# A second cross-attention layer with stacked f16 score operands and f32 value products

## The chip, the cores and the metric

The kernel runs on one core of one Trainium2 chip, in one launch. The metric is the device time of that launch in microseconds (us). The kernel before takes 1686.76 us, the median of three runs from 1685.93 to 1686.81.

## The reference

Four layers, each with a cross-attention and a feed-forward part, act on x of 8 batch items by 256 tokens by 128 numbers. Each part adds its result to x, behind a layer norm. The context has 256 tokens of 96 numbers per batch item. The second layer's attention, which the change rewrites, has 16 heads of 8 numbers each:

```python
q = (q_tokens @ Wq.T).reshape(B, T_q, 16, 8).transpose(0, 2, 1, 3)
k, v = ...                       # the same from kv_tokens, 96 columns wide
attn = softmax(einsum('bhqd,bhkd->bhqk', q, k) / sqrt(8), axis=-1)
out = einsum('bhqk,bhkd->bhqd', attn, v).transpose(0, 2, 1, 3).reshape(B, T_q, 128)
return out @ Wo.T
x = x + _L1_xattn_ref(_layernorm(x), ctx_768, Wq, Wk, Wv, Wo)      # second layer
x = x + _L1_ffn_ref(_layernorm(x), ...)                            # 8 experts, one per token
```

All of it is in f32, and the kernel's f16 operands are pairs of a high and a low part.

## The kernel before, in words

The kernel is one program for each engine: TensorE (PE), VectorE (DVE), ScalarE (ACT), GpSimd (POOL) and SyncE (SP, which issues DMAs). All five walk the same lists of steps, written out by hand, and meet at semaphores (`need`). Layers are numbered from 0, so the second is `ATT[1]` and `FFN[1]`.

**The layer's passes.** `ATT[1]` works through the 8 batch items one after the other. Its kinds of pass are "early" (keys and values of all items, 512 columns at a time, put between the products of the first feed-forward's first chunk by `ffn_schedule`), "prologue" (the first three quarters of the queries), "first" (item 0), "mid" (items 1 to 6, a loop on every engine), "last" (item 7) and "epilogue". The fourth quarter of the queries is filled at head 4 of "first", behind "lastrows", the norm of the last 512 tokens. The first feed-forward has four chunks of 512 tokens and eight experts, and ends just before.

**One head.** `head_steps` gives every engine its order. In step i come the scores of head i, its softmax, the turn of head i-2, the low part of head i-3, the value products of head i-4, and in odd steps the norm of a pair:

```python
st = [("scores", i), ("softmax", i)] if i < 16 else []
st += [("turn", i - 2)] if i < 18 else []
st += [("low", i - 3)] if i < 19 else []
st.append(("av", i - 4))
if i % 2:
    st.append(("norm", (i - 4) // 2))
```

For the scores, PE multiplies the query, masked to the head's 8 rows of 128 (`Qz`, written by POOL in four masks per item, line 1147), with the whole key tile `kT`: two f32 products of 128 rows and 256 columns. DVE takes the negative maximum of each row (`negm`, line 2445), ACT the exponential (`Pm`, line 1491, in two halves). PE turns the four 128x128 blocks (line 1671). ACT copies the turned tile to f16 (`PTh`, line 1445), DVE subtracts that from the tile to get the low part (`PTl`, line 2456), and PE forms the value products in f16 from three pairings, (high, high), (high, low), (low, high): twelve of 9 columns, the ninth column being a one for the sum of the row. DVE divides by that sum (lines 2514 and 2516).

**Between the heads.** `NARROW` puts the previous item's output projection, residual (lines 2535 to 2539), layer norm and the choice and rank of its experts (lines 2594 to 2635) at fixed steps of the item. In "first" eight heads also carry a block maximum over the next feed-forward's weights (line 2336); their maximum (`uprow`, line 2421) goes to POOL, which reduces it over all partitions (line 1110), and DVE picks the result up at head 15 (line 2425). In "last" the weights are split in f16 parts (lines 1445 and 2463). SP loads the biases and weights of the next feed-forwards once the first feed-forward is done (line 917).

Of the kernel before, what the change touches and what calls it, by code (L numbers as in the profile page):

```python
# [9 lines left out]
F16 = mybir.dt.float16  # L10
# [8 lines left out]
P = 128  # L19
B, S, D = 8, 256, 128  # L20
T = B * S
# [39 lines left out]
class AttentionSems:  # L61
    def __init__(self, c):
# [7 lines left out]
        self.ctxb, self.qm, self.ostats, self.onorm = c["ctxb"], c["qm"], c["ostats"], c["onorm"]  # L70
# [156 lines left out]
def att_early(A):  # L227


    if A.dh != 64:  # L230
        return [(kind, j) for kind in "kv" for j in range(4)]
    return [("k", 0), ("k", 1)] + ([] if A.null else [("k", 2)]) + [("v", 0), ("vlow", 0), ("v", 2), ("vlow", 2)]


def att_prologue(A):

    return ([("sums", 0), ("srows", 0), ("tokens", 0)] if A.null else []) + [("q", 0), ("q", 1), ("q", 2)] + (
        [("sn", 0)] if A.null else [])
# [54 lines left out]
def on_act(A, kind, k, m):  # L293

    if A.dh != 64:
# [10 lines left out]
                (5, 1): ("v", 0), (6, 1): ("v", 1), (7, 1): ("v", 2), (8, 1): ("v", 3)}  # L306


def ffn_schedule(F, first):
# [3 lines left out]
    for e in range(F.E):  # L313
        if e * F.FT < F.U:
            for ft in range(F.FT):
                st.append(("up", (e, ft)))
                if F.n == 0 and first and (e, ft) in NEXT_CONTEXT:
                    st.append(("context", NEXT_CONTEXT[e, ft]))
                if F.k and e == 0 and ft == 1:
                    st.append(("gate", 1))  # L320
# [14 lines left out]
def build(nc, a, out):  # L335
    ctx = ExitStack()
    with ctx:
# [21 lines left out]
        headmask = sb("headmask", [P, 16])  # L359
# [43 lines left out]
        vmax = sb("vmax", [P, 4])  # L403
        vmaxall = sb("vmaxall", [P, 4])
# [28 lines left out]
        G = Qz[:, :, :].rearrange("p h s -> p (h s)").rearrange("p (g s) -> p g s", s=CH)  # L433
# [169 lines left out]
        out_written = sem("out_written")  # L603

# [40 lines left out]
        def att_counts(A):  # L645
# [3 lines left out]
            vfills = [m % 2 or A.dh == 64 for k in kinds if A.n != 2 for kind, j, m, _ in steps(A, 0, k) if kind == "v"]  # L649
            return dict(vhigh=sum(vfills), vlow=len(vfills) - sum(vfills), filled=fills, act=(fills + 1) // 2, dve=fills // 2, scores=nh, negmax=nh, exp=nh, dn=8 * B if A.null else 0, onull=8 * B if A.null else 0, xnb=B if A.null else 0,  # L650
                        turn=nh, pt0=nh // 2 if A.n == 2 else nh, pt1=nh // 2 if A.n == 2 else nh, av=nh, norm=nh if A.n == 2 else nh // 2, stats=B,
                        yn=B, numbers=B if A.n == 2 else 0, ctxb=B if A.dh == 64 else 0, qm=4 * B if A.n == 1 else 0,
# [99 lines left out]
        def batches(eng, A, body):  # L752
# [6 lines left out]
            with eng.Fori(1, B - 1) as b:  # L759
                body(b, "mid")  # L760
# [3 lines left out]
        def chunks(eng, F, body, behind_first=None, last=NCH):  # L764
# [3 lines left out]
            with eng.Fori(1, last) as c:  # L768
                body(c, False)

# [44 lines left out]

        def v_low(A, dve, k, src, b):
# [13 lines left out]

        kTall = kT[:, :, :].rearrange("p h s -> p (h s)")

        def keys_of(A, b, h):
            return kTall[:, bass.ts(b, S)] if A.n == 1 else kT[:, h, :]
# [80 lines left out]
        def _(sp):  # L915
# [56 lines left out]
            for n in ROUTED:  # L972
# [4 lines left out]
                for i in range(5):  # L977
                    sp.dma_start(xs[n][27 * P * i:27 * P * (i + 1), D:D + 1].bitcast(U32).rearrange("(t p) o -> p (t o)", p=P),
                                 unused[:, 27 * i:27 * i + 27], allow_slow_non_contiguous=True).then_inc(rows_set[n], 16)
            need(sp, ffn_s[0].y, NCH * FFN[0].E)  # L980
            load("b2", b2all, a["L1_ffn_b2"].rearrange("(o e) d -> o (e d)", o=1).to_broadcast([P, 8 * D]))
# [4 lines left out]
            load("l2f", n2, a["L2_ffn_w2"].rearrange("e d f -> d e f"))  # L986

# [50 lines left out]
        def _(pool):  # L1038
# [21 lines left out]
            for e in range(8):  # L1060
# [12 lines left out]
            link(pool.memset(headmask[:, :], 1.0))  # L1073
            link(pool.affine_select(out=headmask[:, :], in_=headmask[:, :], compare_op=ALU.is_ge, fill=0.0,
                                    base=0, pattern=[[-8, 16]], channel_multiplier=1))
            link(pool.affine_select(out=headmask[:, :], in_=headmask[:, :], compare_op=ALU.is_ge, fill=0.0,
                                    base=7, pattern=[[8, 16]], channel_multiplier=-1))
# [19 lines left out]
            pool.partition_all_reduce(vmaxall[:, 0:3], vmax[:, 0:3], P, RMAX).then_inc(setup_vmaxall, 1)  # L1097
# [36 lines left out]
            def attention(A, last_rows=None):  # L1134
# [6 lines left out]
                def masks(b, bw, heads=range(0, 16, 4)):  # L1141

                    for h in heads:
                        if b is not None:
                            need(pool, s.scores, b * 16 + (h + 4))
                        plain(pool)
                        pool.tensor_tensor(  # L1147
                            Qz[:, h:h + 4, :], xnT[:, bass.ts(bw, S)].unsqueeze(1).to_broadcast([P, 4, S]),
                            headmask[:, h:h + 4].unsqueeze(2).to_broadcast([P, 4, S]), ALU.mult).then_inc(s.qm.sem, 1)

                def body(b, kinds):
                    if A.n == 2:
# [13 lines left out]
                        pool.memset(R1[:, 5632:5648], 0.0)  # L1166
                        for c in range(3):
# [38 lines left out]
                    if A.n == 1 and kinds == "prologue":  # L1206

                        need(pool, s.ring.act, 5)
                        need(pool, ffn_s[0].y, NCH * FFN[0].E)
                        masks(None, 0, (0, 4))  # L1210
                        last_rows()
                        masks(None, 0, (8, 12))
# [11 lines left out]
                    if A.n == 1 and kinds == "first":  # L1224

                        need(pool, s.ring.act, 6)
                        need(pool, s.ring.dve, 6)
                        masks(0, 1)
# [1686 lines left out]
```

## Time and profile before

| | |
|---|---|
| runs | 1686.76 us median, 1685.93 to 1686.81 |
| the profiled execution | 1684.98 us, its span 1683.2 us |
| PE, its weight loads, DVE, ACT, POOL busy | 1401.7, 1083.9, 1133.7, 833.0, 396.2 us |
| granted clock, mean | 0.929 of full speed |
| the second layer's attention | about 578 to 890 us |
| one middle item of it | 33.7 us |

The span is the time from the first to the last instruction on the chip; the execution has 1.8 us around it. PE's clock has two levels, 1.2 and 2.4 GHz, and the profile gives the granted clock of a stretch as a share of the higher, so 0.50 is the lower level throughout. Busy shares of the whole span mix stages with different limits. The stage that counts here is the second layer's attention, and the rows below are mostly from it.

### The profile page before, as it was taken

The page shows a single profiled execution, that of the slowest core. Times are in us where ns is not written, and L with a number is a line of the kernel's source. Part 1 is how long each engine was busy: PE and PEld are TensorE (multiplying, and loading weights), DVE is VectorE, ACT ScalarE, POOL GpSimd, SP SyncE. Part 2 cuts the span into 40 slices and gives each one's busy share as a digit, 9 for nine tenths or more (in the row PEclk, how much of TensorE's full clock was granted, in tenths as well). Part 3 has the DMA queues.
Part 4 walks back from the last instruction along what each step waited for, and adds up shares of the span by engine and source line. Part 5 has one row for each costly group of instructions (what it writes and reads, how often), then busy time and mean ns, then how long its engine had stood idle before and what let it go on. Part 6 is the DMA issues. An engine that isn't in the chain of part 4 may idle for free. (4 is left out here: it accounts for less than half of the span.)

```text
span 1683.2 us, 38856 instructions
## 1 busy us (share of the span) xinstructions
PE 1401.7 (83%) x12529; PEld 1083.9 (64%) x12529; DVE 1133.7 (67%) x3284; ACT 833.0 (49%) x1838; POOL 396.2 (24%) x738
## 2 busy tenths in 40 slices
PE   3899999978999979998966864488868899898977
PEld 2677777765666658777754644366646677677665
DVE  4788888876766668888865454443357877788851
ACT  1666666654333346666642242322246665656633
POOL 2000000011111223433322324643311222222221
PEclk9999999988999989999978877699988999999989
DMA  8999100000000210000001100131110000000000
GB/s 228 279 98 132 0 0 0 0 1 1 1 1 0 68 49 5 3 3 6 4 4 43 35 27 17 41 102 43 35 52 1 2 0 0 0 0 0 1 1 25
DMA packets 109759, 55.06 MB, mean 33 GB/s; under 512 B 44593, under 2 KB 102578, under 8 KB 109474
## 3 DMA queue, kind: packets, MB, share of 16 engines
q1 hardware_dynamic: 106146, 46.53, 15.0%
q0 software_dynamic: 3520, 7.31, 1.3%
q8 instruction: 55, 0.90, 0.2%
q14 instruction: 38, 0.31, 0.1%
HBM read 27.09 MB, written 26.74 MB: 32 GB/s over the span
## 5 line engine op out<-in xcount | busy, mean ns | idle before, releaser
L1491 ACT ACTIVATE Pm<-bank,negm 128x256 f32<-128x256 f32 x528 | 220.8, 470 | 220.3 <-DVE negm L2445 122.6
L1667 PE MATMUL bank<-kT,Qz 64*128 64x256 f32 (+2 forms) x1568 | 309.6, 414 | 16.5 <-DVE negm L2436 4.7
L1671 PE MATMUL bank<-ident,Pm 128*128 128x128 f32 x1568 | 238.0, 288 | 63.6 <-DVE PTs L2456 58.3
L2456 DVE TENSOR_TENSOR PTs<-bank,PTs 128x512 f16<-128x512 f32 x384 | 251.4, 682 | 39.7 <-ACT PTs L1445 38.9
L1671 PEld LDWEIGHTS bank<-ident,Pm 128*128 128x128 f32 x1568 | 181.1, 146 | 140.9 <-issue 95.3
L1667 PEld LDWEIGHTS bank<-kT,Qz 64*128 64x128 f32 (+1 forms) x1568 | 189.7, 194 | 99.2 <-issue 57.4
L1445 ACT ACTIVATE PTs<-bank 128x512 f16<-128x512 f32 (+1 forms) x388 | 215.5, 590 | 3.8 <-PE bank L1671 3.7
L1667 PEld LDWEIGHTS bank<-VxF,PTs 128*128 128x128 f16 (+1 forms) x4672 | 183.3, 100 | 11.6 <-DVE PTs L2456 3.2
L1667 PE MATMUL bank<-VxF,PTs 128*128 128x65 f16 (+3 forms) x4672 | 187.4, 189 | 2.1 <-DVE PTs L2456 1.9
L1491 ACT ACTIVATE Pm<-Pm,negm 128x256 f32<-128x256 f32 x256 | 109.7, 497 | 117.2 <-DVE negm L2436 90.0
L2445 DVE TENSOR_REDUCE negm<-bank 128x2 f32<-128x512 f32 x136 | 93.5, 688 | 47.5 <-PE bank L1667 44.2
L1667 PE MATMUL bank<-Qz,R 128*128 128x128 f16 x978 | 93.1, 235 | 22.3 <-ACT Qz L1445 13.7
L2436 DVE CUSTOM_DVE_ANT_0 Pm<-bank,mb 128x256 f32<-128x256 f32 x256 | 93.5, 420 | 18.7 <-PE bank L1667 17.9
L1667 PEld LDWEIGHTS bank<-Qz,R 128*128 x978 | 71.7, 102 | 48.9 <-issue 37.0
L2442 DVE TENSOR_REDUCE negm<-bank 128x2 f32<-128x512 f32 x128 | 88.1, 689 | 19.9 <-PE bank L1667 18.9
L1667 PE MATMUL bank<-xHL,R 128*128 (+1 forms) x432 | 99.5, 379 | 1.4 <-DVE Qz L2850 1.2
L1147 POOL TENSOR_TENSOR Qz<-xnT,headmask 128x1024 f32<-128x1024 f32 x32 | 60.7, 1899 | 161.9 <-PE bank L1667 123.2
L1667 PE MATMUL bank<-xnT,R 128*128 (+2 forms) x288 | 87.3, 433 | 8.1 <-DVE VxF L820 6.1
L1667 PEld LDWEIGHTS bank<-R,Qz 128*128 128x128 f32 x704 | 83.8, 192 | 11.1 <-ACT Qz L1643 6.4
L1636 ACT ACTIVATE Pm<-bank,upback 128x512 f32<-128x512 f32 x72 | 49.4, 687 | 82.3 <-PE bank L1667 77.1
L1667 PE MATMUL bank<-R,Qz 128*128 128x128 f32 x704 | 85.0, 276 | 3.1 <-ACT Qz L1643 3.1
L1378 POOL DMA_INDIRECT expert_rows_by_token<-PTs,Qz x62 | 60.6, 977 | 110.3 <-DVE PTs L2764 66.6
(331 smaller groups left out, 2160.5 us busy)
## 6 DMA issues: line engine op xcount, KB each, us to landing
token_rows_by_expert<-trash SPq DMA_DIRECT2D x10, 1782.0 KB, 18.6
Qz<-token_rows_by_expert SPq DMA_DIRECT2D x62, 66.0 KB, 1.8
R<-expert_rows_by_token SPq DMA_DIRECT2D x12, 256.0 KB, 4.6
R<-in_L_ffn_ew SPq DMA_DIRECT2D x2, 1024.0 KB, 7.3
R<-in_L_ffn_w SPq DMA_DIRECT2D x1, 2048.0 KB, 9.5
R<-in_L_xattn_Wkv SPq DMA_DIRECT2D x2, 768.0 KB, 6.4
R<-in_L_ffn_w SPq DMA_DIRECT2D x1, 1408.0 KB, 12.2
R<-in_L_xattn_Wq SPq DMA_DIRECT2D x2, 512.0 KB, 3.9
```

The source lines that it names most:

```text
L1147: pool.tensor_tensor(Qz[:, h:h + 4, :], xnT[:, bass.ts(bw, S)].unsqueeze(1).to_broadcast([P, 4, S]), headmask[:, h:h + 4].unsqueeze(2).to_ ...
L1378: pool.indirect_dma_start(out=ytok[F.n], out_offset=bass.IndirectOffsetOnAxis(ap=xb2[:, i % RING, D:D + 1].bitcast(U32), axis=0), in_=yb2[ ...
L1445: return act.activation(dst, src, ACT.Copy, scale=1.0 if gain is None else gain)
L1491: last = act.activation(masked, masked if A.mask == "full" else bank[k % 2][:, qt * S:(qt + 1) * S], ACT.Exp, bias=negm[:, k % 4, qt:qt + ...
L1636: act.activation(sg[0:M, u % 2, :], bank[u % 2][0:M, :], ACT.Silu, scale=upback[0:M, F.n:F.n + 1]).then_inc(s.silu.sem, 1)
L1667: return pe.matmul(o, l, r, start=start, stop=stop)
L1671: return pe.transpose(o, i, ident[0:n, 0:n])
L2436: last = dve.tensor_tensor_reduce(Pm[:, k % 4, qt * S:(qt + 1) * S], v[:, qt, :], mb0[:, qt, :], -1.0, -LOWEST, ALU.add, ALU.min, nm[:, qt ...
L2442: chain(dve.tensor_reduce(nm, v, AX.X, ALU.max, negate=True))
L2445: dve.tensor_reduce(nm, v, AX.X, ALU.max, negate=True).then_inc(s.negmax.sem, 1)
L2456: dve.tensor_tensor(PTl[:, k % 4, :], bank[2 + k % 2][:, :], PTh[:, k % 4, :], ALU.subtract).then_inc(s.pt[1].sem, 1)
```

## The change

**Scores.** Queries and keys are scaled, and split into a high and a low f16 part each, by ACT (high) and DVE (low) as they leave PE's banks. Per head the 8 rows of k high, k high, k low stand above one another, 24 in all, against q high, q low, q high, so that one f16 product of 24 rows makes the sum of three. Head k stands at partitions 32 (k mod 4) on. The parts get there through DRAM: SP writes each tile's parts out (`head_rows`) and reads them back in twelve DMAs of 8 partitions (`in_bands`). POOL's masks are gone. The scale is undone in the exponential, whose `scale` is now a column of a tile, and in `negm`, which becomes a reduction and a multiplication by that column that waits for it.

**Where the fills stand.** The three query fills of the prologue move into the last chunk of the first feed-forward, whose loop is written out for that chunk on all engines. The gelu tile `G` of that feed-forward moves from `Qz`, where the bands now arrive, to `R0`. The keys of heads 8 to 15 stand in a part of `R0` that is free only when the first feed-forward ends. PE's loop over the middle items is written out six times.

**Values.** V stays in f32. ACT copies the turned exponentials of even heads in f32, DVE those of odd heads, and PE forms four f32 products of 9 columns. A turn waits for the copy of the head two before it, which used the same bank.

```diff
+NEXT_QUERIES = {(3, 0): ("q", 0), (4, 0): ("q", 1), (5, 0): ("q", 2)}
+            for c in range(NCH):
+                head_rows_written("k", c)
+            sp.wait_ge(head_rows_out["k"], 16 * NCH)
+            in_bands(bandsk[0], "k", slice(0, 2), slice(0, T), key_bands[0])
+            for c in range(3):
+                head_rows_written("q", c)
+                sp.wait_ge(head_rows_out["q"], 16 * (c + 1))
+                in_bands(bandsq, "q", slice(0, 4), slice(c * CH, (c + 1) * CH), query_bands[0])
             need(sp, ffn_s[0].y, NCH * FFN[0].E)
+            in_bands(bandsk[1], "k", slice(2, 4), slice(0, T), key_bands[1])
             load("b2", b2all, a["L1_ffn_b2"].rearrange("(o e) d -> o (e d)", o=1).to_broadcast([P, 8 * D]))
...
+            head_rows_written("q", 3)
+            sp.wait_ge(head_rows_out["q"], 16 * 4)
+            in_bands(bandsq, "q", slice(0, 4), slice(3 * CH, T), query_bands[1])
...
-            pool.partition_all_reduce(vmaxall[:, 0:3], vmax[:, 0:3], P, RMAX).then_inc(setup_vmaxall, 1)
+            pool.partition_all_reduce(vmaxall[:, 0:6], vmax[:, 0:6], P, RMAX).then_inc(setup_vmaxall, 1)
...
-                    if A.n == 1 and kinds == "mid":
-                        masks(b, b + 1, (0, 4))
...
+                            factor = headscale[:, 2:3] if A.n == 1 else -1.0 if A.mask == "full" else 1.0
...
-                                                      scale=-1.0 if A.mask == "full" else 1.0)
+                                                      scale=factor)
...
+                        elif kind == "turn" and A.n == 1 and k % 2 == 0:
+                            need(act, s.turn, b * nh + (k + 1))
+                            need(act, s.av, b * nh + (k - 3))
+                            move(PTs[:, k % 4, :], bank[2][:, :]).then_inc(s.pt[0].sem, 1)
...
-                            if A.n == 1 and k % 4 == 0:
-                                need(pe, s.qm, b * 4 + (k // 4 + 1))
+                            if A.n == 1 and kinds == "first" and k in (0, 8):
+                                pe.wait_ge(key_bands[k // 8], 16 * 12)
+                                if k == 0:
+                                    pe.wait_ge(query_bands[0], 16 * 36)
+                            if A.n == 1 and kinds == "mid" and b == 1 and k == 0:
+                                pe.wait_ge(query_bands[1], 16 * 12)
...
+                                if A.n == 1:
+                                    rows, j = slice(32 * (k % 4), 32 * (k % 4) + 24), k // 4
+                                    last = mm(o, bandsq[rows, j, b * S + qt * P:b * S + (qt + 1) * P],
+                                              bandsk[j // 2][rows, j % 2, b * S:(b + 1) * S])
...
+                                need(pe, s.pt[k % 2], b * (nh // 2) + k // 2)
...
+                            elif A.n == 1:
+                                need(pe, s.pt[k % 2], b * (nh // 2) + (k // 2 + 1))
+                                p = k // 2
+                                if k % 2 == 0:
+                                    need(pe, s.norm, b * 8 + (p - 1))
+                                for qt in range(2):
+                                    r = (k % 2) * 2 + qt
+                                    for kt in range(2):
+                                        last = mm(bank[4 + p % 2][:, r * P:r * P + 9],
+                                                  PTs[:, k % 4, kt * S + qt * P:kt * S + (qt + 1) * P],
+                                                  Vhead(A, b if k >= 0 else b - 1, kt, k % 16, VxF), kt == 0, kt == 1)
...
+                dve.tensor_reduce(vmax[:, 4:5], w1nat[:, 0:128], AX.X, ALU.max, apply_absolute_value=True)
+                dve.tensor_reduce(vmax[:, 5:6], w1nat[:, 128:224], AX.X, ALU.max, apply_absolute_value=True)
...
+                            elif A.n == 1:
+                                chain(dve.tensor_reduce(rowmax[:, k % 4, :], v, AX.X, ALU.max, negate=True))
+                                dve.tensor_scalar(nm, rowmax[:, k % 4, :], headscale[:, 2:3], None,
+                                                  ALU.mult).then_inc(s.negmax.sem, 1)
...
+                            elif k % 2:
+                                need(dve, s.turn, b * nh + (k + 1))
+                                need(dve, s.av, b * nh + (k - 3))
+                                move(PTs[:, k % 4, :], bank[3][:, :]).then_inc(s.pt[1].sem, 1)
```

What this does to the order on PE, in a middle item, before (`kT`, `Qz` are the score operands, `Pm` the exponentials, `PTs` the turned ones, `VxF` the values):

```order
L1667 MATMUL bank<-kT,Qz 128x256 x2
L1671 MATMUL bank<-ident,Pm 128x128 x4
L1667 MATMUL bank<-VxF,PTs 128x9 x12
L1667 MATMUL bank<-kT,Qz 128x256 x2
L1671 MATMUL bank<-ident,Pm 128x128 x4
L1667 MATMUL bank<-VxF,PTs 128x9 x12
```

And the same engine in the kernel after:

```order
L1714 MATMUL bank<-kT,Qz 128x256 x2
L1718 MATMUL bank<-ident,Pm 128x128 x4
L1714 MATMUL bank<-VxF,PTs 128x9 x4
L1714 MATMUL bank<-kT,Qz 128x256 x2
L1718 MATMUL bank<-ident,Pm 128x128 x4
L1714 MATMUL bank<-VxF,PTs 128x9 x4
```

The order of the three kinds stays; the score products have become f16 with 24 rows (which this listing doesn't show), and of twelve value products four are left.

DVE in the same place, two heads of a middle item, before (`negm` is the negative maximum, `rden` and `On` belong to the norm; register operations issue addresses):

```order
L2445 TENSOR_REDUCE negm<-bank 128x2
L2456 TENSOR_TENSOR PTs<-bank,PTs 128x512
L670 REGISTER_ALU
L2445 TENSOR_REDUCE negm<-bank 128x2
L2456 TENSOR_TENSOR PTs<-bank,PTs 128x512
L2514 RECIPROCAL rden<-bank 128x4
L2516 TENSOR_TENSOR On<-bank,rden 128x2x2x8
```

And after (`rowmax` is the maximum before its scale):

```order
L2521 TENSOR_REDUCE rowmax<-bank 128x2
L2481 ISA
L2522 TENSOR_SCALAR negm<-rowmax,headscale 128x2
L694 REGISTER_ALU x2
L2283 COPY PTs<-bank 128x512
L694 REGISTER_ALU
L2521 TENSOR_REDUCE rowmax<-bank 128x2
L2481 REGISTER_ALU
L2522 TENSOR_SCALAR negm<-rowmax,headscale 128x2
L2608 RECIPROCAL rden<-bank 128x4
L2481 REGISTER_ALU
L2610 TENSOR_TENSOR On<-bank,rden 128x2x2x8
```

A subtraction in every head has become a copy in every second head, and each reduction has a second operation behind it that needs its result.

SP between the loads of the start and those of the next feed-forwards, after; before, the first of these rows was followed at once by the last three:

```order
L1008 DMA token_rows_by_expert<-unused 128x27x1 x5
L1018 DMA head_rows_k<-On 256x1x512 x4
L1025 DMA kT<-head_rows_k 8x2x2048 x12
L1018 DMA head_rows_q<-xnT 256x1x512
L1025 DMA Qz<-head_rows_q 8x4x512 x12
...
L1025 DMA R<-head_rows_k 8x2x2048 x12
L947 DMA R<-in_L_ffn_b 128x1024
L947 DMA R<-in_L_ffn_w 128x22x128 x2
L947 DMA R<-in_L_ffn_w 128x8x352
```

Twelve band DMAs now stand on this queue ahead of each use, those of the later keys between the end of the first feed-forward and the loads.

## Rows read from the trace of the kernel before

**Rows 1.** Stretches: length, busy us (x), PE PEld DVE ACT POOL, clock, DMA, GB/s.
```profile
700.00:734.00 34.00, 30.83 (x340) 26.44 (x338) 27.62 (x70) 21.63 (x51) 12.66 (x12) 0.95 0.01 4
850.00:855.00 5.00, 3.51 (x42) 2.70 (x41) 4.18 (x8) 3.62 (x9) 1.49 (x3) 1.00 0.00 0
660.00:664.00 4.00, 4.00 (x30) 3.30 (x27) 2.61 (x6) 2.65 (x6) 0.34 (x1) 0.57 0.05 17
```

**Rows 2.** Timeline of PE, one head of a middle batch: start, duration, instruction.
```profile
712.33 1.11 PE L1667 MATMUL bank<-kT,Qz 128*128 x4
713.28 0.60 PE L1671 MATMUL bank<-ident,Pm 128*128 128x128 f32 x4
713.72 0.45 PE L1667 MATMUL bank<-VxF,PTs 128*128 x12
714.02 1.11 PE L1667 MATMUL bank<-kT,Qz 128*128 x4
```

**Rows 3.** Timeline of DVE beside it, [idle before <-releaser].
```profile
712.21 0.69 DVE L2456 TENSOR_TENSOR PTs<-bank,PTs 128x512 f16<-128x512 f32 x1 [0.20 <-ACT PTs L1445]
712.82 0.17 DVE L2514 RECIPROCAL rden<-bank 128x4 f32<-128x4 f32 x1
713.03 0.19 DVE L2516 TENSOR_TENSOR On<-bank,rden 128x32 f32<-128x32 f32 x1
```

**Rows 4.** Group: ACT copies (busy us, mean ns); line 2634 (min/median/max ns).
```profile
L1445 ACT ACTIVATE PTs<-bank 128x512 f16<-128x512 f32 x17 | 10.2, 598 | 0.0
...
L2634 DVE TENSOR_TENSOR rk<-ohacc x8: 161/1880/1887, 655.7 to 885.6; 128x8 f32<-128x8 bf16 x8
```

**Rows 5.** Timeline of DVE, POOL and DVE, end of the first batch.
```profile
607.62 0.16 DVE L2421 TENSOR_REDUCE uprow<-upmax 128x1 f32<-128x8 f32 x1
...
622.52 0.38 POOL L1110 PARTITION_ALL_REDUCE uprowall<-uprow  x1 [6.08 <-issue]
...
624.79 0.69 DVE L2445 TENSOR_REDUCE negm<-bank 128x2 f32<-128x512 f32 x1
```

**Rows 6.** Timeline of PE, one expert of the first feed-forward.
```profile
566.97 2.75 PE L1667 MATMUL bank<-xHL,R 128*128 x12
569.56 1.95 PE L1667 MATMUL bank<-R,Qz 128*128 128x128 f32 x16
```

**Rows 7.** Timeline of PE, small f32 products at either clock level.
```profile
717.59 0.59 PE L1667 MATMUL bank<-gw,OT 128*128 128x8 f32 x4
718.03 1.11 PE L1667 MATMUL bank<-kT,Qz 128*128 x4
...
858.53 1.00 PE L1667 MATMUL bank<-gw,OT 128*128 128x8 f32 x4 [1.26 <-ACT OT L1445]
859.38 2.05 PE L1667 MATMUL bank<-kT,Qz 128*128 128x256 f32 x4
```

**Rows 8.** Timeline of DVE in the fourth layer, reduction and dependent operation.
```profile
1455.05 0.69 DVE L2442 TENSOR_REDUCE negm<-bank 128x2 f32<-128x512 f32 x1 [0.38 <-PE bank L1667]
1455.78 0.16 DVE L2443 TENSOR_TENSOR negm<-negm,nsn 128x2 f32<-128x2 f32 x1
1455.94 0.69 DVE L2442 TENSOR_REDUCE negm<-bank 128x2 f32<-128x512 f32 x1
```

**Rows 9.** Groups of the page: busy, mean ns, idle before.
```profile
L1636 ACT ACTIVATE Pm<-bank,upback 128x512 f32<-128x512 f32 x72 | 49.4, 687 | 82.3 <-PE bank L1667 77.1
```

**Rows 10.** Timeline of PE at the start of the second layer.
```profile
577.55 2.84 PE L1667 MATMUL bank<-xnT,w1T 128*128 128x512 f32 x6
```

**Rows 11.** Timeline of SP; DMA issues of the page (KB, us to landing).
```profile
11.04 0.43 SPq L917 DMA_DIRECT2D OT<-in_L_xattn_Wo  x1
...
Qz<-token_rows_by_expert SPq DMA_DIRECT2D x62, 66.0 KB, 1.8
```

**Rows 12.** Timeline of PE, third layer's turns; and a later stretch.
```profile
1072.54 3.65 PE L1671 MATMUL bank<-ident,R 128*128 128x128 f32 x16
...
1077.50:1080.00 2.50, 1.14 (x7) 0.67 (x7) 2.47 (x6) 0.66 (x2) 2.03 (x4) 1.00 0.10 36
```

More of the change, by code:

```diff
@@ L235, in att_prologue @@
 def att_prologue(A):
+    if A.n == 1:
+        return []
     return ([("sums", 0), ("srows", 0), ("tokens", 0)] if A.null else []) + [("q", 0), ("q", 1), ("q", 2)] + (
@@ L648, in att_counts @@
             fills = sum(s[0] in FILLS for k in kinds for s in kind_steps(A, k))
[L649 to L652, printed above, removed]
+            vfills = sum(s[0] == "v" for k in kinds for s in kind_steps(A, k)) if A.dh == 64 else 0
+            halves = nh if A.dh == 64 else nh // 2
+            return dict(vhigh=vfills, vlow=0, filled=fills, act=(fills + 1) // 2, dve=fills // 2, scores=nh, negmax=nh, exp=nh, dn=8 * B if A.null else 0, onull=8 * B if A.null else 0, xnb=B if A.null else 0,
+                        turn=nh, pt0=halves, pt1=halves, av=nh, norm=nh if A.n == 2 else nh // 2, stats=B,
+                        yn=B, numbers=B if A.n == 2 else 0, ctxb=B if A.dh == 64 else 0, headhigh=8 if A.n == 1 else 0, headlow=4 if A.n == 1 else 0,
                         ostats=B if A.null else 0, onorm=B if A.null else 0)
@@ L758, in batches @@
             body(0, "first")
-            with eng.Fori(1, B - 1) as b:
-                body(b, "mid")
+            if A.n == 1 and eng is nc.tensor:
+                for b in range(1, B - 1):
+                    body(b, "mid")
+            else:
+                with eng.Fori(1, B - 1) as b:
+                    body(b, "mid")
             body(B - 1, "last")
@@ L767, in chunks @@
                 behind_first()
-            with eng.Fori(1, last) as c:
+            with eng.Fori(1, last - (F.n == 0 and last == NCH)) as c:
                 body(c, False)
+            if F.n == 0 and last == NCH:
+                body(NCH - 1, False)
         att_s = [AttentionSems(c) for c in
@@ L1139, in attention @@
                 start = count[0]
[L1141 to L1149, printed above, removed]
                 def body(b, kinds):
@@ L1613, in body @@
                 def body(c, first):
-                    for kind, k in ffn_schedule(F, first):
+                    for kind, k in ffn_schedule(F, first, isinstance(c, int) and c == NCH - 1):
                         if kind == "context":
@@ L2007, in early_read @@
             def early_read(A):
-                need(pe, att_s[A.n].ring.act, (sum(step[0] in FILLS for step in att_early(A)) + 1) // 2)
-                need(pe, att_s[A.n].ring.dve, sum(step[0] in FILLS for step in att_early(A)) // 2)
+                need(pe, att_s[A.n].ring.act, 4)
+                need(pe, att_s[A.n].ring.dve, 4)
             def routed_by_token(F):
@@ L2121, in body @@
                     xc = xnT[:, bass.ts(c, CH)]
-                    for kind, k in ffn_schedule(F, first):
+                    for kind, k in ffn_schedule(F, first, isinstance(c, int) and c == NCH - 1):
                         if kind == "context":
```

150 lines of the change are left out of this document (97 added, 53 removed).

## The prediction

> **What bounds the kernel now.** I first read the busy time by stretch. In a middle batch of the second layer's attention (700 to 734 us; six of the eight batches run such a pass, 33.7 us each) TensorE is busy for 30.8 of 34 us at a granted clock of 0.95, VectorE for 27.6, ScalarE for 21.6 and POOL for 12.7 [rows 1]. Then TensorE's timeline: one head costs 1.69 us, 0.95 for the two f32 score products, 0.44 for the four turns and 0.30 for the twelve f16 value products, with no idle time between them [rows 2]. So a middle batch is bound by TensorE, and VectorE stands close behind: 0.61 for the subtraction that makes the low part and 0.4 for the two small operations of the norm every second head [rows 3], to which the reduction of the scores adds about 0.6. Last I read the wait at the end of the first batch: the row maximum for the next feed-forward's scale is there at 607.6, POOL's all-reduce of it runs only at 622.5, 6.08 us after the end of POOL's previous instruction, and the first reduction of batch 1 starts at 624.8 [rows 5]. VectorE's queue stands behind that all-reduce, and through it ScalarE's and TensorE's.
>
> **The change, TensorE.** Per head two f32 score products go and two f16 ones of 256 columns come. Twelve f16 products of 512 columns start 2.59 us before what follows them, 0.216 each [rows 6]; half the columns is 0.11, so 0.22 for the two against 0.95. That a product has 24 rows instead of 128 I count at nothing: no row shows a product of fewer rows, and I bound it by 0.22 and the 0.30 of twelve short f16 products. The turns stay at 0.44. Twelve f16 value products become four f32 ones of 9 columns: four of 8 columns take 0.44 to the next instruction at full clock [rows 7], so +0.14. A head falls from 1.69 to 1.10, and a batch to 17.6 us and some 2 us of narrow fills. TensorE stops being the bound, if it keeps its clock.
>
> **VectorE.** The subtraction in every head becomes a copy of the same tile from the same bank in every second head, for which I take the same 0.61 (0.30 per head). The reduction is followed by a small scaling that waits for it: in the fourth layer, where such a pair exists, 0.73 and 0.16 [rows 8], so 0.89 per head. With the norm's 0.20 per head that is 1.39, against 0.61 + 0.6 + 0.20 = 1.41 before. Nothing is won there, and VectorE becomes the bound. What is not per head is 27.62 - 16 x 1.21 - 8 x 0.40 = 5.1 us of a batch; 1.89 of it is one tiny operation, L2634, whose eight instances take 0.16 to 1.89, most of them the long end [rows 4]. The masks of POOL run beside it and go; for it alone I take the short end, 0.17, so 3.4 remain, 4.5 with the gaps between small dependent operations.
>
> **ScalarE.** It loses half of its copies, 8 x 0.60 [rows 4], and its exponentials take their scale from a tile. A ScalarE pass over 128x512 with such a scale takes 0.687 [rows 9] against the copy's 0.598, +0.09; for 32 of them +2.9. About 20 us per batch: not the bound, unless an exponential costs twice as much.
>
> **The hand-off.** The pitch is set by a loop over two heads. When VectorE has copied an odd head, TensorE can turn the next odd head and form the value products of the copied one (0.06 + 0.44 + 0.44, with the scores about 1.1); only then can VectorE do the norm. In between VectorE has only one softmax step (0.8), so it waits some 0.3; then norm 0.4, softmax 0.89, copy 0.61. That gives 3.0 to 3.2 per two heads, 1.5 to 1.6 per head, 24.3 to 25.4 per batch. With the 4.5 and half a microsecond of small waits a middle batch takes about 30.0, against 33.7: 6 x 3.7 = **-22**. The bounds are VectorE without any hand-off (16 x 1.39 + 4.5 = 26.7, -42) and no gain at all.
>
> **First batch.** POOL's masks go. The maximum itself does not come much earlier, since in the eight heads with a block maximum VectorE is full before and after (1.39 + 0.6 against 1.41 + 0.6); the start of the layer gives about 2 us, because the last quarter of the queries comes in before the heads pile up. So the maximum stands at about 605.6, the all-reduce, with the 6.08 that preceded it kept in full, ends at about 612.1, and head 15 arrives at about 611.6 (four heads of 1.5 later). The wait of 8 us shrinks to under 1, and batch 1 starts at about 613.7: **-11** (-9 to -12; the better end if those 6.08 need not be paid once POOL has been free for long).
>
> **Last batch and the start.** The last batch gains as a middle one does: **-4** (0 to -6). The three query fills, 2.84 [rows 10], leave the head of the layer for the last feed-forward chunk; TensorE does them either way, so I count 0, and up to +2 where they push the chunk's last products. Two more small reductions in the set-up and five tiny scale operations: **+0.4**, an estimate, since each is shorter than the 0.69 of a 512-column reduction [rows 8] and partly beside loads. The bands come through DRAM: an issue on SP takes about 0.43 and a 66 KB transfer lands 1.8 us later [rows 11], so twelve issues and the landing are 5 to 7 us. In the last chunk the first query fill stands at about 550 and three series, each with a write of 2 us ahead, take 21 to 27 us: done by 571 to 577. They are needed from 580.4 (577.55 + 2.84) on. The last quarter's bands wait on SP behind the expert weights' loads, which I put at 605; with one series they are there at 611 to 612, needed at 613.7. I count 0; the cover is thin (below).
>
> **The sum.** -22 - 11 - 4 + 0.4 = -36 or -37. The profiled execution took 1684.98 (span 1683.2 and 1.8 around it), so 1649 for it; the median of the runs shown is 1686.76, 1.8 above, so I forecast **1651**.
>
> **Rivals.**
> *The clock alternates.* TensorE is now idle in a third of each batch. At the lower level (0.50, 1.2 GHz) four small f32 products took 0.85 instead of 0.44 [rows 7]; by that ratio a head costs 0.43 + 0.86 + 0.85 = 2.14, more than VectorE's 1.55. For it: at 660 to 664 the clock stood at 0.57, near the lower level. Against it: in the last batch, at 3.51 busy of 5 us, the share that I expect, it stood at 1.00 [rows 1]. With a third of the heads at the lower level a middle batch takes (2 x 30 + 38.2) / 3 = 32.7, so 6 x (-1.0) - 11 + 0 = about **1670**. The turns are now the largest f32 block of TensorE's work. In the trace sixteen turns alone ran at 0.228 each, the lower level, and the clock stood at 1.00 shortly after, with nothing else in between [rows 12]. The Trainium skill, "TensorE: Matmul & The Clock Gate", "Part 4: PE-mode transpose", says that full clock does not engage for turns; by that rule this rival would be the likeliest and its time the forecast. The rows disagree with it here.
>
> *Only the wait goes.* The hand-off costs as much as TensorE gave up, middle batches stay at 33.7: 1686.8 - 11 - 1 = **1675**. For it: VectorE's own work per head is unchanged. Against it: it idles 6.4 of 34 us now, and L2634's 1.7 goes.
>
> *Bands late.* The write of the rows, twelve issues and the landing are in series three times in the last chunk, and the last quarter waits behind the expert weights' loads on SP. A miss costs up to one such series, 5 to 6 us: **1657**.
>
> *Slower.* TensorE stays at the lower level for the whole attention: 16 x 2.14 + 4 of narrow fills at that level = 38.2 per middle batch, 6 x 4.6 = +27, last batch +4, less the 11: about **1706**. It decides against the change once more than two thirds of the heads run at that level (30 + 8.2 x 0.67), that is, when middle batches exceed 35.5 us and their loss, 6 x 1.8, eats the 11. For it: at 660 to 664 TensorE was busy for all four us and the clock stood at 0.57; against it, the row of the last batch, and that TensorE would then be busy without a pause, as it is in the stretches of before that run at 0.95.
>
> **Chances.** Forecast 52% (its own range 1638 to 1660, from a pitch between VectorE alone and 1.7 per head), alternating clock 25%, bands late 9%, only the wait goes 7%, low clock throughout 7%. The range 1632 to 1680 leaves out the slower case and a little on either side. A measurement of this kernel tells about 0.2% (3.4 us) from no change. The first four cases are all faster; I leave 3% of them for mixtures that end within 0.2%: faster 0.90, same 0.03, slower 0.07.
>
> **What would show it.** Right: scores to turns 0.2 to 0.25 apart and four value products in 0.44; idle time of TensorE put down to VectorE's copy; VectorE's busy time near 26 of 30 us; L2634 at 0.17; no wait over 1 us for the all-reduce; b = 1's first reduction near 614; granted clock over 0.9. Wrong: middle batches over 32 us, a granted clock under 0.85 in them, turns at 0.86, or TensorE's first scores released by a DMA.

## The result and the profile after

The changed kernel takes 1816.96 us, the median of four runs from 1816.17 to 1819.52, against 1686.78 for the kernel before beside it: a ratio of 1.077 (95% interval 1.076 to 1.079). The forecast was 1651 and a range up to 1680. It is 8% slower, on the other side of the forecast and worse than the rival that had named this side (1706).

The page of the kernel after, its busy times of TensorE and the granted clock in 40 slices of the span, in tenths:

```profile
PE 1569.7 (87%) x11761; PEld 1228.3 (68%) x11761; DVE 1118.6 (62%) x3342; ACT 830.5 (46%) x1778; POOL 335.7 (19%) x705
...
PEclk9999999989999555555555697769997999999989
```

The clock stands at half from the fourteenth slice to the twenty-second, which is the second layer's attention. By stretch (length, busy us of PE, PEld, DVE, ACT, POOL, granted clock, DMA share, GB/s), the last chunk of the first feed-forward, the attention's first heads, and a stretch of middle items:

```profile
535.00:580.00 45.00, 44.80 (x277) 29.85 (x278) 30.09 (x88) 19.68 (x27) 4.36 (x6) 1.00 0.16 45
590.00:600.00 10.00, 8.98 (x45) 6.09 (x43) 4.38 (x11) 3.80 (x7) 0.00 (x0) 0.66 1.01 224
700.00:760.00 60.00, 60.00 (x276) 51.15 (x276) 29.21 (x87) 23.53 (x47) 5.12 (x8) 0.50 0.01 3
```

Where [rows 1] have 30.83 of 34 us at 0.95, TensorE is now busy for 60.00 of 60 at 0.50, and VectorE for half of the time. TensorE is the bound, without a pause, at 1.2 GHz. Its timeline (start, duration, instruction) shows the first scores, the first wait, and further on the same head at both levels:

```profile
579.95 0.39 PE L1714 MATMUL bank<-kT,Qz 24*128 24x256 f16 x4
585.20 0.60 PE L1714 MATMUL bank<-kT,Qz 24*128 24x256 f16 x2 [4.85 <-ACT Pm L1525]
```

```profile
597.56 0.39 PE L1714 MATMUL bank<-kT,Qz 24*128 24x256 f16 x2
597.88 0.66 PE L1718 MATMUL bank<-ident,Pm 128*128 128x128 f32 x4
598.37 0.96 PE L1714 MATMUL bank<-VxF,PTs 128*128 128x9 f32 x8
599.37 0.39 PE L1714 MATMUL bank<-kT,Qz 24*128 24x256 f16 x2
600.76 1.09 PE L1718 MATMUL bank<-ident,Pm 128*128 128x128 f32 x4 [1.00 <-DVE PTs L2283]
601.64 1.72 PE L1714 MATMUL bank<-VxF,PTs 128*128 128x9 f32 x8
603.29 0.60 PE L1714 MATMUL bank<-R,Qz 24*128 24x256 f16 x2
603.82 1.11 PE L1718 MATMUL bank<-ident,Pm 128*128 128x128 f32 x4
604.73 1.72 PE L1714 MATMUL bank<-VxF,PTs 128*128 128x9 f32 x8
```

From 597.56 to 599.37 the clock was at its full level: scores 0.32 to the turns, turns 0.49, and the value products 1.00 to the next scores. After a wait of 1.00 for VectorE's copy the scores take 0.53, the turns 0.88 to 0.91, and the value products 1.65: 3.09 us a head. These rows answer to [rows 2], where a head took 1.69. And they show a second thing: the four f32 value products stand there as **eight** records, as the two f32 score products of [rows 2] stand as four.

VectorE (two steps of a middle item, with the idle time and its releaser), and the first all-reduce behind the maximum of the weights:

```profile
703.21 0.69 DVE L2521 TENSOR_REDUCE rowmax<-bank 128x2 f32<-128x512 f32 x1 [1.54 <-PE bank L1714]
703.93 0.23 DVE L2522 TENSOR_SCALAR negm<-rowmax,headscale 128x2 f32<-128x2 f32 x1
705.76 0.18 DVE L2608 RECIPROCAL rden<-bank 128x4 f32<-128x4 f32 x1 [1.60 <-PE bank L1714]
```

```profile
612.65 0.16 DVE L2497 TENSOR_REDUCE uprow<-upmax 128x1 f32<-128x8 f32 x1
612.95 0.38 POOL L1165 PARTITION_ALL_REDUCE uprowall<-uprow  x1 [25.16 <-DVE uprow L2497]
```

The scaling starts 0.72 behind the reduction and takes 0.23, where [rows 8] had 0.73 and 0.16. The small operation L2728, which was L2634, takes 0.16 in all of its eight instances, and the all-reduce starts 0.30 behind the maximum, where [rows 5] had 14.9. From 640 to 960 us VectorE waits for TensorE 65 us ahead of the 49 reciprocals, one in every second head, and 58 us ahead of the 98 reductions.

Where the 131.2 us between the two spans (1683.2 and 1814.4) lie, by the start of the residual of each item (lines 2535 and 2629): the first comes at 640.78 before and at 654.50 after, +13.7; from there to the seventh 204.9 and 314.6, +109.7 (a middle item 33.97 and 52.45); from the seventh to the last 30.0 and 37.5, +7.5; the rest of the kernel +0.2.

### The profile page after: what moved, and what is told of

The parts are those of the page before. It is cut to its first block and busy times, and to the rows that moved or that the text cites. A ratio compares the mean times of both kernels' runs of the same rounds, so it can differ in the third digit from the quotient of the medians.

```text
span 1814.4 us, 36910 instructions
## 1 busy us (share of the span) xinstructions
PE 1569.7 (87%) x11761; PEld 1228.3 (68%) x11761; DVE 1118.6 (62%) x3342; ACT 830.5 (46%) x1778; POOL 335.7 (19%) x705
## 5 line engine op out<-in xcount | busy, mean ns | idle before, releaser
L1714 PEld LDWEIGHTS bank<-VxF,PTs 128*128 128x128 f16 (+1 forms) x4160 | 356.4, 158 | 8.9 <-DVE PTs L2537 2.5
L1714 PE MATMUL bank<-VxF,PTs 128*128 128x65 f16 (+2 forms) x4160 | 346.5, 234 | 1.8 <-DVE PTs L2537 1.7
L1525 ACT ACTIVATE Pm<-bank,negm,headscale 128x256 f32<-128x256 f32 x256 | 130.6, 561 | 230.1 <-DVE negm L2522 209.3
L1714 PE MATMUL bank<-kT,Qz 64*128 64x256 f32 (+2 forms) x1184 | 199.6, 413 | 17.2 <-ACT Pm L1525 6.9
L2537 DVE TENSOR_TENSOR PTs<-bank,PTs 128x512 f16<-128x512 f32 x256 | 164.0, 682 | 34.3 <-ACT PTs L1478 34.0
L1714 PEld LDWEIGHTS bank<-kT,Qz 64*128 64x128 f32 (+2 forms) x1184 | 106.3, 183 | 95.1 <-issue 57.3
L1525 ACT ACTIVATE Pm<-bank,negm 128x256 f32<-128x256 f32 x272 | 113.6, 470 | 116.6 <-DVE negm L2519 75.5
L1525 ACT ACTIVATE Pm<-Pm,negm 128x256 f32<-128x256 f32 x256 | 109.7, 497 | 117.1 <-DVE negm L2512 89.9
L2521 DVE TENSOR_REDUCE rowmax<-bank 128x2 f32<-128x512 f32 x128 | 88.4, 690 | 74.8 <-PE bank L1714 69.1
L1714 PE MATMUL bank<-Qz,R 128*128 128x128 f16 x978 | 93.7, 234 | 22.5 <-ACT Qz L1478 13.7
L2518 DVE TENSOR_REDUCE negm<-bank 128x2 f32<-128x512 f32 x128 | 88.1, 688 | 20.8 <-PE bank L1714 19.0
L1714 PE MATMUL bank<-xHL,R 128*128 128x512 f16 (+1 forms) x432 | 100.0, 379 | 0.9 <-DVE R L2944 0.6
L2608 DVE RECIPROCAL rden<-bank 128x4 f32<-128x4 f32 x128 | 22.9, 179 | 110.0 <-PE bank L1714 109.7
```

The source lines that it names most:

```text
L1525: last = act.activation(masked, masked if A.mask == "full" else bank[k % 2][:, qt * S:(qt + 1) * S], ACT.Exp, bias=negm[:, k % 4, qt:qt + ...
L1714: return pe.matmul(o, l, r, start=start, stop=stop)
L2518: chain(dve.tensor_reduce(nm, v, AX.X, ALU.max, negate=True))
L2521: chain(dve.tensor_reduce(rowmax[:, k % 4, :], v, AX.X, ALU.max, negate=True))
L2537: dve.tensor_tensor(PTl[:, k % 4, :], bank[2 + k % 2][:, :], PTh[:, k % 4, :], ALU.subtract).then_inc(s.pt[1].sem, 1)
L2608: chain(dve.reciprocal(rd, o[:, :, :, A.dh]))
```

## The experiments

Two questions had to be told apart: what took the clock, and what the parts cost at a given clock. In the tables, "middle item" is the distance between the residuals of two middle items, and "clock" is the granted clock of 700 to 740 us. The kernels before and after, hold_f16_768 and hold_f16_timed, which is hold_f16 once more, have four runs each. The others have one, beside 1683 to 1685 us for the kernel before on the same chip. In every trace the clock stands at 1.00 from 405 to 580 us, ahead of this stage. The code is shortened: "twice over" is an operand that is read twice, for 256 columns.

| kernel | us | middle item | clock |
|---|---|---|---|
| before | 1686.8 | 33.97 | 0.96 |
| after | 1817.0 | 52.45 | 0.50 |
| scores_only | 1696.1 | 36.30 | 0.50 |
| values_only | 1703.0 | 37.33 | 1.00 |
| fill24 / fill128 | 1872.2 / 1873.1 | 59.3 / 59.5 | 0.50 |
| no_scale | 1684.2 | 35.15 | 0.50 |
| no_scale_fill_f16 | 1720.6 | 40.3 | 0.50 |
| no_scale_fill_f32 | 1683.3 | 31.03 | 1.00 |
| no_scale_fill_f32_24 | 1797.7 | 49.8 | 0.50 |
| after_hold | 1766.4 | 37.45, up to 806 us | 1.00 |
| after_burst | 1818.5 | 52.46 | 0.50 |
| hold256 | 1661.7 | 31.05 | 1.00 |
| hold128 | 1744.3 | 42.69 | 0.50 |
| hold_f16 (hold_f16_timed) | 1657.8 (1656.9) | 30.43 | 1.00 |
| hold_f16_24 | 1785.6 | 46.84 | 0.50 |
| hold_f16_768 | 1750.4 | 43.68 | 0.50 |

**One part alone.** scores_only keeps the stacked f16 scores and puts the value products back; values_only does the reverse, on the kernel before.

```diff
# scores_only, in the value products
-  mm(..., PTs[:, k % 4, ...], Vhead(..., VxF), kt == 0, kt == 1)
+  for n, (pp, vv) in enumerate(((PTh, VxH), (PTh, VxL), (PTl, VxH))):
+      mm(..., pp[:, k % 4, ...], Vhead(..., vv), kt == 0 and n == 0, kt == 1 and n == 2)
# values_only, in the same place: the other way round
```

> Stacked f16 scores as in the changed kernel, value products as before (f16 copy by ScalarE, low part by VectorE in every head, twelve f16 products). Theory A (the f32 value products with their weight loads are what holds the clock at the lower level): granted clock back over 0.9 between 640 and 820 us, a head's scores, turns and values at 0.32, 0.49 and 0.30, VectorE the bound with 0.89 + 0.61 + 0.20 per head, middle batches about 32 to 33 us, about 1665 us in all. Theory B (the small f16 score products are what takes the clock, whatever the values do): clock near 0.50, a head at 0.53 + 0.91 + 0.37 = 1.81, middle batches about 35 us, about 1690 us.

> Scores and masks as before, values in f32 from one copy as in the changed kernel. Both theories: each f32 product shows as two records, so the eight take about 0.96 us at full clock against 0.30 for the twelve f16 ones. Theory A: clock near 0.50, a head at 1.8 + 0.9 + 1.64 = 4.3, middle batches about 80 us, over 1980 us in all. Theory B: the f32 scores keep the clock at 1.00, a head at 0.95 + 0.44 + 0.96 = 2.35, middle batches about 44 us, about 1760 us.

The stretch 700 to 740 us of scores_only, then of values_only, then a head of values_only (start, duration):

```profile
700.00:740.00 40.00, 37.06 (x342) 26.99 (x340) 32.40 (x93) 27.92 (x57) 5.10 (x8) 0.50 0.01 4
```

```profile
700.00:740.00 40.00, 39.68 (x296) 36.48 (x294) 26.23 (x66) 17.90 (x42) 14.98 (x14) 1.00 0.01 3
```

```profile
714.29 0.96 PE L1677 MATMUL bank<-VxF,PTs 128*128 x8
715.10 1.11 PE L1677 MATMUL bank<-kT,Qz 128*128 x4
716.05 0.60 PE L1681 MATMUL bank<-ident,Pm 128*128 128x128 f32 x4
716.49 0.96 PE L1677 MATMUL bank<-VxF,PTs 128*128 x8
```

Theory B held in the clock: the f16 scores alone lose it, whatever the values do, and the f32 scores alone keep it at 1.00, with the new value products beside them. The values have a price of their own: 0.81 to the next instruction in place of [rows 2]'s 0.30, 37.33 per middle item. The time expected for values_only, 1760 us, was 57 too long: sixteen heads at its 2.35 are 37.6, and not the 44 that it has for a middle item. Measured were 0.95 + 0.44 + 0.81 = 2.20 a head and 37.33. TensorE's pauses are not what decides: scores_only and the changed kernel sit at 0.50 while it is busy for 37 of 40 us or for all of them.

**More f16 work ahead of the scores, on few and on all rows.** Two f16 products of a constant tile, 256 columns each, into the scores' bank, which the scores overwrite; 24 rows in fill24 (`full` is the head's own 24 rows), 128 in fill128.

```diff
+  for qt in range(2):
+      mm(bank[k % 2][:, qt * S:(qt + 1) * S], onesb[full, :], onesb[full, :] twice over)
```

> The changed kernel with two more f16 products of 24 rows and 256 columns of constants ahead of each head's scores, into the same bank, which the scores then overwrite. If more streamed columns are enough for the clock: clock near 1.00, a head at 1.81 + 0.22 = 2.03, middle batches about 37 us, about 1705 us. If the clock stays at 0.50: a head at 3.09 + 0.43 = 3.5, middle batches about 60 us, about 1870 us.

> As fill24, but the two added products have 128 rows. If the rows in use count for the clock and 24 are too few: clock near 1.00 here and not in fill24, about 1705 us. If rows make no difference: the same clock and time as fill24.

Both stayed at 0.50 and cost 55 and 56 us more than the changed kernel, the price of the added products at the lower level. This pair could not tell rows from columns, since neither side came up.

**The scale taken out, and f32 work added.** no_scale is scores_only with constant scales in the parts, no second operation behind the reduction and no scale column in the exponential. On it stand the same f16 products (no_scale_fill_f16), and one f32 product of the identity with 256 columns, of 128 rows (no_scale_fill_f32) and of 24 (no_scale_fill_f32_24).

```diff
+  full = slice(0, P)                       # _24: slice(32 * (k % 4), 32 * (k % 4) + 24)
+  mm(bank[k % 2][:, 0:S], ident[full, :], ident[full, :] twice over)
```

> Stacked f16 scores, value products as before, and the per-head scale taken out (constant scales in the parts of q and k, no second operation behind the reduction, no scale column in the exponential). Theory A, as far as it is left (the chain behind the reduction cost the clock, by making TensorE wait): clock over 0.9, VectorE the bound with 0.6 + 0.61 + 0.20 per head, middle batches about 29 us, about 1650 us. Theory B (the short f16 score products do not hold the clock, whatever waits): clock 0.50, a head at 0.53 + 0.91 + 0.44 = 1.88 on TensorE, middle batches about 34 us, about 1690 us.

> no_scale with two f16 products of 128 rows and 256 columns of constants ahead of each head's scores. Theory B, if any more streamed work in place of the lost f32 products will do: clock near 1.00, TensorE 1.33 per head, VectorE the bound, middle batches about 29 us, about 1650 us. Theory B', only f32 products do: clock 0.50, a head at 2.3, middle batches about 41 us, about 1735 us.

> no_scale with one f32 product of 128 rows and 256 columns of the identity ahead of each head's scores: half of the f32 score work of the kernel before. Theory B: clock near 1.00, TensorE 1.11 + 0.47 = 1.58 per head, a little over VectorE's 1.4, middle batches 31 to 32 us, about 1660 us. If half is not enough: clock 0.50, a head at 1.88 + 0.95 = 2.8, middle batches about 49 us, about 1800 us.

> As no_scale_fill_f32 with 24 rows in place of 128 in the added product. If rows in use do not count for the clock: same time and clock. If they do: clock 0.50 here and 1.00 there.

The stretch of no_scale and one of its heads:

```profile
700.00:740.00 40.00, 38.17 (x356) 28.31 (x352) 30.23 (x79) 25.29 (x59) 5.08 (x8) 0.50 0.01 4
```

```profile
709.44 0.60 PE L1710 MATMUL bank<-R,Qz 24*128 24x256 f16 x2
709.97 1.11 PE L1714 MATMUL bank<-ident,Pm 128*128 128x128 f32 x4
710.88 0.51 PE L1710 MATMUL bank<-VxF,PTs 128*128 128x9 f16 x12
711.32 0.60 PE L1710 MATMUL bank<-R,Qz 24*128 24x256 f16 x2
```

That of no_scale_fill_f16:

```profile
700.00:740.00 40.00, 40.00 (x338) 25.69 (x337) 26.46 (x69) 21.78 (x50) 5.09 (x8) 0.50 0.01 4
```

Those of no_scale_fill_f32 before and after its clock rose, and then that of no_scale_fill_f32_24:

```profile
620.00:640.00 20.00, 20.00 (x139) 12.14 (x138) 9.78 (x23) 9.29 (x21) 0.26 (x1) 0.50 0.01 2
660.00:680.00 20.00, 18.64 (x217) 12.84 (x215) 16.73 (x47) 14.03 (x33) 2.29 (x2) 1.00 0.03 9
```

```profile
700.00:740.00 40.00, 40.00 (x276) 28.52 (x274) 22.19 (x60) 17.30 (x40) 5.09 (x8) 0.50 0.01 4
```

The last two kernels differ in nothing but the rows of one product per head; the 24 rows are those of the head's own scores, so they change place from head to head. At the lower level both run at the same pace, 139 records of TensorE in 20 us and 276 in 40, so the added product costs the same time. With 24 rows the clock never leaves 0.50 in this stage; with 128 it comes up, at 655, and stays up through the middle items, to 846. TensorE's timeline at the rise shows what it did just before:

```profile
653.18 1.20 PE L1710 MATMUL bank<-w1T,OT 128*128 128x128 f32 x4
654.17 1.06 PE L1710 MATMUL bank<-ident 128*128 128x256 f32 x2
655.16 0.41 PE L1710 MATMUL bank<-R,Qz 24*128 24x256 f16 x2
655.50 0.66 PE L1714 MATMUL bank<-ident,Pm 128*128 128x128 f32 x4
656.00 0.45 PE L1710 MATMUL bank<-VxF,PTs 128*128 128x9 f16 x12
```

Four more 128-row f32 records, the output projection, stand between two heads; behind them the turns take 0.50 in place of 0.91. Because the rise came so late, the kernel took 1683.3 us and not the 1660 expected. In no_scale the taking out of the scale made 1.15 us of a middle item (36.30 to 35.15) and nothing for the clock: theory A, as far as it was left, fell. no_scale_fill_f16 limits what its rows alone can explain: it adds two f16 products of the scores' own 256 columns on all 128 rows, and in the middle items the clock stayed at 0.50.

**A start at full clock.** The changed kernel's TensorE waits 4.85 us for the first exponentials. after_burst puts ten 128-row f32 products there and nothing else; after_hold adds the f32 product of 128 rows to each head as well.

```diff
+  if A.n == 1 and kinds == "first" and k == 2:
+      for _ in range(10): mm(bank[2][:, 0:S], ident, ident twice over)
```

> The changed kernel with one f32 product of 128 rows and 256 columns of the identity ahead of each head's scores (overwritten by them), and ten such products while TensorE waits for the first exponentials. If work of 128 rows is what the clock misses: granted clock near 1.00, a head at 1.81 + 0.6 = 2.4, middle batches about 43 us, about 1760 us, faster than the changed kernel though TensorE does a third more. If the short f32 value products also hold the clock down: 0.50, a head at 3.09 + 1.13 = 4.2, about 1950 us.

> The changed kernel with only the ten f32 products in the wait for the first exponentials. If the wait was the cause: clock 1.00 from the first heads on and held, a head at 1.81, middle batches about 34 us, about 1680 us. If the heads' own work loses the level: 0.50 within the first batch, about 1815 us as the changed kernel.

after_burst, from its start to 640 us:

```profile
580.00:590.00 10.00, 8.97 (x55) 6.73 (x54) 8.13 (x24) 3.60 (x9) 4.34 (x6) 1.00 0.54 80
590.00:600.00 10.00, 8.79 (x42) 6.19 (x41) 5.26 (x12) 4.73 (x10) 0.00 (x0) 0.61 0.99 197
600.00:640.00 40.00, 40.00 (x183) 34.34 (x183) 21.86 (x54) 16.68 (x33) 0.64 (x2) 0.50 0.29 89
```

after_hold, in the middle items and late in the stage:

```profile
700.00:740.00 40.00, 39.69 (x295) 30.43 (x293) 27.12 (x84) 21.79 (x45) 5.08 (x8) 1.00 0.01 4
820.00:840.00 20.00, 20.00 (x81) 15.35 (x80) 7.18 (x17) 6.93 (x14) 0.00 (x0) 0.50 0.00 0
```

A warm start alone is lost within the first heads, and the kernel takes as long as without it. With the product in every head, the changed kernel does more work on TensorE and takes 50.6 us less (1817.0 to 1766.4). Its level fell once more at 806 us and, but for a short rise near 847, stayed down to the end of the stage; why there, no run shows. The 1760 us expected came near this by luck: the middle items at 1.00 took 37.45 and not 43, and the fall of the level took the gain back.

**How little will do, and a version faster than before.** On no_scale, with the warm start: one f32 product of 256 columns (hold256) or of 128 (hold128), two f16 products of 512 columns (hold_f16), the same on 24 rows (hold_f16_24), and one of 512 and one of 256 (hold_f16_768); more of them in the last item (hold256, too, has two there, where no_scale_fill_f32 has one).

```diff
+  for _ in range(4 if kinds == "last" else 2):
+      mm(bank[k % 2], onesb[:, :], onesb[:, :] four times over)       # hold_f16
```

> no_scale_fill_f32 with ten more such products while TensorE waits for the first exponentials, and two per head instead of one in the last batch. If the clock stays up once it is up: 1.00 from the first heads on, middle batches 31.0 us as there, the 75 us at the lower level gone: about 1655 us. If the level falls by itself in the first batch: about 1680 us.

> As hold256 with half the columns in the added product (three per head in the last batch). If the clock holds: TensorE 1.11 + 0.3 per head, VectorE the bound, middle batches about 29 us, about 1640 us. If it doesn't: 0.50, a head at 1.88 + 0.5, middle batches about 41 us, about 1730 us.

> As hold256 with two f16 products of 128 rows and 512 columns in place of the f32 one. If f16 work counts as f32 work of the same duration: clock 1.00, TensorE 1.11 + 0.43 per head, about 1650 us. If only f32 work counts: 0.50, a head at 1.88 + 0.86, middle batches about 48 us, about 1780 us.

> hold_f16 with its two added products per head on 24 rows in place of 128; the same columns, the same ten 128-row f32 products at the start. If rows in use count: the clock falls to 0.50 within the first batch and stays, a head at 1.88 + 0.86, about 1780 us. If only time or columns count: the 1658 us of hold_f16.

> hold_f16 with 768 columns per head in place of 1024 (three products of 512 and one of 256 in the last batch). If the clock holds: TensorE 1.11 + 0.32 per head, middle batches about 29 us in place of 30.4, about 1648 us. If not: 0.50, a head at 1.88 + 0.65, about 1760 us.

> hold_f16 again, timed: 1655 to 1661 us, ratio to the kernel before about 0.983.

The same stretch of hold128, hold_f16, hold_f16_24 and hold_f16_768, in this order:

```profile
700.00:740.00 40.00, 40.00 (x317) 29.56 (x318) 25.38 (x63) 20.41 (x47) 5.09 (x8) 0.50 0.01 4
700.00:740.00 40.00, 36.20 (x442) 22.42 (x438) 34.17 (x100) 27.21 (x63) 7.17 (x10) 1.00 0.02 7
700.00:740.00 40.00, 40.00 (x294) 24.65 (x292) 22.37 (x58) 19.09 (x44) 2.75 (x5) 0.50 0.01 4
700.00:740.00 40.00, 40.00 (x314) 23.95 (x313) 25.05 (x66) 19.93 (x46) 5.09 (x8) 0.50 0.02 5
```

A head of hold_f16:

```profile
712.31 0.59 PE L1710 MATMUL bank<-onesb 128*128 128x512 f16 x2
712.84 0.39 PE L1710 MATMUL bank<-kT,Qz 24*128 24x256 f16 x2
713.15 0.66 PE L1714 MATMUL bank<-ident,Pm 128*128 128x128 f32 x4
713.65 0.46 PE L1710 MATMUL bank<-VxF,PTs 128*128 128x9 f16 x12
713.97 0.59 PE L1710 MATMUL bank<-onesb 128*128 128x512 f16 x2
```

hold_f16 and hold_f16_24 again differ in rows alone, in f16 this time and both from a warm start: 1.00 and 0.50, 1657.8 and 1785.6 us. So at the same streamed columns the rows in use decide, in f32 and in f16, from a cold start and from a warm one. In each pair the 24 rows also change place from head to head; a filler on 24 fixed rows, or on a number of rows in between, was not run. Rows are not all that counts: with less added work on the same 128 rows, hold_f16_768 (timed: 1750.35 us, ratio 1.040, 1.036 to 1.044) and hold128 fell to 0.50 as well, so neither cheaper filler served. hold_f16, timed, takes 1656.9 us, a ratio of 0.984 (0.981 to 0.986) to the kernel before: stacked f16 scores with constant scales, the old value products, and products whose result nobody reads.

## Why the prediction was wrong

**The clock (the condition "if it keeps its clock", and the step "That a product has 24 rows instead of 128 I count at nothing").** This is the step that failed. The forecast put nothing down for what the change of the scores does to the clock, and left it to rivals, 25% for a clock that alternates and 7% for the lower level throughout. In time the new scores cost little more than was worked out (0.32 for two where 0.22 was taken and 0.30 was the bound), but the f32 scores were the work that held the clock: without them it stands at 0.50 (scores_only), with them and the new values at 1.00 (values_only). A filler of 24 rows neither brings the level back (f32) nor keeps it (f16), where the same filler of 128 rows does. How much of the loss is due to the 24 rows and how much to the shorter products is open: no run had f16 scores on 128 rows, and no_scale_fill_f16, and hold_f16_768 from a warm start, suggest that these, too, would have lost the clock. The forecast argued against the lower level by the row of the last batch, 3.51 busy of 5 us at 1.00 [rows 1]. That row had the f32 scores in it, as TensorE's timeline of the kernel before shows:

```profile
851.88 1.11 PE L1667 MATMUL bank<-kT,Qz 128*128 128x256 f32 x4
```

Its other argument, that TensorE would then be busy without a pause, was wrong as well: by its records TensorE is busy for 60 of 60 us at 0.50. The Trainium skill, "TensorE: Matmul & The Clock Gate", "Why this matters for your kernels", advises to keep TensorE busy without gaps for full clock; this trace disagrees.

**The f32 value products (the term +0.14).** Four of 8 columns were read as 0.44 [rows 7], but the kernel forms two products there, each of which shows as two records: the count x4 is of records. At full clock the four take 0.81 (values_only), at the lower level 1.65. This would have been cheap alone, since TensorE's 0.32 + 0.49 + 0.81 = 1.62 per head is near the 1.5 to 1.6 that the forecast had through VectorE. At the lower level it is not: the low-clock rival's 38.2 us per middle item took 0.85 for them, and 16 x (1.65 - 0.85) = 12.8 of the 14.3 us that it lacks of 52.45.

**The turns.** The Trainium skill, "TensorE: Matmul & The Clock Gate", "Part 4: PE-mode transpose", says that full clock does not engage for them; the prediction held [rows 12] against it. [rows 12] show the full level only in a stretch that begins 1.3 us behind the end of the sixteen turns. The stretch between, in the kernel before, has 0.62 for its mean:

```profile
1075.00:1077.50 2.50, 1.19 (x6) 0.79 (x4) 2.33 (x8) 1.58 (x3) 1.89 (x3) 0.62 0.13 46
```

That mean puts the rise at about 1076.9, 0.7 us behind the end of the turns, and TensorE did nothing in between. This speaks for the forecast's reading, but in the 5 us ahead of the turns it had small products too. In no_scale the turns are the longest part of a head (0.91 of 1.88) and the clock stays at 0.50, which agrees with the page. No run was made to tell what turns count for.

**VectorE, ScalarE, POOL, the bands.** These steps were right, or nearly so, in size: 0.72 for the reduction against 0.73, 0.23 for the scaling against 0.16, 0.16 for L2728 against 0.17, and an exponential of 561 ns where it was 470 (+0.09). The all-reduce followed at once, the better end of its bounds. The first scores started at 579.95, right behind the feed-forward's last product, and no wait of TensorE in this stage is put down to a DMA, so no band was late.

**The hand-off.** The forecast's 30.0 for a middle item could not be checked: no run brought the changed kernel's clock up without added work. From after_hold an estimate is to be had: 37.45 less 16 added products of 0.61 is 27.7 for TensorE, under the forecast's 30.0, so VectorE's loop could then have decided.

What stays open: why after_hold lost its level at 806 us, what the turns count for, and how rows and the length of the products share in the loss.

## What to carry to other kernels

Before cutting TensorE's work, ask which of its instructions hold its clock. In these runs it was enough work over all 128 rows, and not busy time. Stacking operands in few rows saves instructions and may cost the clock for the whole stage; if the engine then has room, products that nobody reads can buy it back: 26 us here (no_scale's 1684.2 to hold_f16's 1657.8), or 50.6 us in the changed kernel. Too little of them only costs time (1744.3 and 1750.4). And when a price is read from a group of f32 products, remember that its count is of records, two for each product.

## What the runs showed that was not expected

The same heads can run at either level. no_scale_fill_f32 ran its first 72 us or so at 0.50 and the rest of its middle items at 1.00 with the same work in each head. The ten products of hold256 at the start took that loss away: the first residual comes at 631.5 in place of 654.6, and the kernel takes 1661.7 in place of 1683.3. An f32 weight load of the value products took this long in the changed kernel (busy, mean ns):

```profile
L1714 PEld LDWEIGHTS bank<-VxF,PTs 128*128 128x128 f32 x144 | 32.9, 334 | 0.0
```

With eight of them per head the loads are busy for 32.9 us of these 60 (700 to 760), about as long as the products, 1.65 of each 3.09 us; the products have only nine columns.
